# An attention and FFN kernel: the first loads in halves on two queues, and the first weight fold ahead of the transposes

## The reference

```python
x = L0_attn_X                                  # (4, 1024, 256)
xn = (x - mean) / sqrt(var + 1e-5)
s = attention(xn, Wq, Wk, Wv, Wo)              # 16 heads of 16, rope, causal softmax
x1 = fwht(xn * SU_ug) / 64                     # Walsh-Hadamard over 256
x_up = x1 @ W_up.T * (Wscale_ug[:1024] * 64)
x_gate = x1 @ W_gate.T * (Wscale_ug[1024:] * 64)
h = fwht(silu(x_gate) * x_up * SU_dp) / 64     # over 1024
g = silu(h @ W_down.T * (Wscale_dp * 64))
out = x + s * g
```

## Time and profile before

| | |
|---|---|
| median of 3 runs | 826.0 us (824.46 to 828.24) |
| the profiled execution | 825.88 us |
| its span, first to last instruction | 824.1 us |
| TensorE busy | 785.3 us, 95% |
| VectorE, ScalarE, GpSimd busy | 563.7, 497.7, 416.8 us |
| HBM read, written | 57.54, 36.95 MB |

### The profile page before, as it was taken

How to read it: one execution, slowest core, us unless ns; L and a number is a source line. 1 busy time by engine, 2 the same in 40 slices (tenths; PEclk the granted TensorE clock), 3 DMA queues, 4 the chain that set the end, 5 groups by cost and what they waited for, 6 DMA issues and landing times.

```text
span 824.1 us, 14501 instructions
## 1 busy us (share of the span) xinstructions
PE 785.3 (95%) x5212; PEld 479.7 (58%) x5212; DVE 563.7 (68%) x1019; ACT 497.7 (60%) x684; POOL 416.8 (51%) x474
## 2 busy tenths in 40 slices
PE   3999999999998999999999999999999999999987
PEld 2678888888765555554555555555555555554435
DVE  3785555445367777777777777777777777776736
ACT  2455475363543667666676765777766677666562
POOL 4569848476580553411665434166453236745233
PEclk9999999999999999999999999999999999999999
DMA  9144442463541221333334453334344333445121
GB/s 322 52 154 128 154 157 78 142 183 131 192 93 52 54 76 53 103 92 118 84 86 118 132 170 99 92 106 128 105 119 139 98 103 98 123 127 182 50 95 58
DMA packets 61055, 95.71 MB, mean 116 GB/s; under 512 B 10360, under 2 KB 27448, under 8 KB 60984
## 3 DMA queue, kind: packets, MB, share of 16 engines
q1 hardware_dynamic: 59400, 92.94, 37.2%
q10 hardware_dynamic: 1584, 1.84, 0.7%
HBM read 57.54 MB, written 36.95 MB: 115 GB/s over the span
## 4 chain that ended last, share of the span: by engine, by line
PE 62%; DVE 5%; POOL 2%; ACT 1%; DMA 1%; issue 1%; SPq 0%; DVEq 0%; ACTq 0%; POOLq 0%
PE ps L1361 15%; PE ps L327 12%; PE ps L1339 11%; PE ps L1316 10%; PE ps L337 7%; PE ps L1402 3%; DVE ps L1615 2%; PE ps L1327 2%; DVE mx L1620 2%; POOL a_sb L382 1%; DMA scr_heads<-o_raw 1%; ACT y_sb L362 1%; DVE y_sb L374 1%; DMA q_s<-shift 0%; ACT a_sb L347 0%
## 5 line engine op out<-in xcount | busy, mean ns | idle before, releaser
L1504 ACT ACTIVATE probs<-ps 128x1024 f32<-128x1024 f32 (+1 forms) x320 | 291.5, 937 | 108.2 <-PE ps L1339 106.4
L1620 DVE TENSOR_REDUCE mx<-ps 128x4 f32<-128x512 f32 (+1 forms) x192 | 215.5, 1134 | 76.9 <-PE ps L1316 48.1
L1199 POOL TENSOR_SCALAR_AFFINE_SELECT probs<-probs 128x256 f32<-128x256 f32 (+1 forms) x192 | 92.8, 486 | 262.1 <-ACT probs L1504 261.0
L1615 DVE CUSTOM_DVE_ANT_0 ps<-ps,tri 128x384 f32<-128x384 f32 (+1 forms) x256 | 154.6, 647 | 30.8 <-PE ps L1316 30.4
L1361 PE MATMUL ps<-probs,v_ones 128*32 128x512 f32 (+3 forms) x1584 | 158.1, 489 | 0.3
L1339 PE MATMUL ps<-q_s,k_s 64*128 64x512 f32 (+3 forms) x768 | 143.5, 399 | 8.1 <-DVE mx L1615 2.3
L1316 PE MATMUL ps<-k_s,q_s 48*128 48x512 f32 (+3 forms) x768 | 137.2, 382 | 3.4 <-DVE mx L1620 1.6
L1339 PEld LDWEIGHTS ps<-q_s,k_s 64*128 64x128 f32 x768 | 68.2, 185 | 104.8 <-issue 69.0
L1316 PEld LDWEIGHTS ps<-k_s,q_s 48*128 48x128 f32 x768 | 69.3, 184 | 70.9 <-ACT probs L1504 50.0
L327 PE MATMUL ps<-xh,wug_hi 128*128 128x512 f32 x256 | 105.7, 413 | 3.7 <-DVE rot L850 1.9
L382 POOL TENSOR_TENSOR a_sb<-a_sb,u_sb 128x512 f32<-128x512 f32 x64 | 83.2, 1307 | 40.3 <-ACT u_sb L355 21.5
(11 more groups left out here) (145 smaller groups left out, 1050.7 us busy)
## 6 DMA issues: line engine op xcount, KB each, us to landing
scr_qk<-kinds SPq DMA_DIRECT2D x64, 256.0 KB, 2.5
q_s<-scr_qk SPq DMA_DIRECT2D x64, 128.0 KB, 2.8
k_s<-scr_qk SPq DMA_DIRECT2D x64, 128.0 KB, 3.0
scr_heads<-o_raw SPq DMA_DIRECT2D x30, 256.0 KB, 2.1
x_sb<-in_x SPq DMA_DIRECT2D x8, 512.0 KB, 5.5
scr_v<-v_st SPq DMA_DIRECT2D x16, 256.0 KB, 2.9
q_s<-scr_qk SPq DMA_DIRECT2D x64, 64.0 KB, 3.0
k_s<-scr_qk SPq DMA_DIRECT2D x64, 64.0 KB, 3.0
```

The lines of the kernel that those rows point to most:

```text
L1199: pool.affine_select(out=part, in_=part, compare_op=ALU.is_ge, fill=0.0, base=0, pattern=pattern, channel_multiplier=-1).then_inc(cut, 1)
L1504: act.activation(probs[:, n % 2, p, :, 0:w], ps[:, bank:bank + 2, 0:w], ACT.Exp, scale=SCALE).then_inc(exp_ok, 1)
L1615: last = dve.tensor_tensor_reduce(part_of, part_of, sh.tri[:, CH - w:CH], 1.0, LOWEST, ALU.add, ALU.max, mx[:, v % 2, kind, h, i % TPC:i % ...
L1620: last = dve.tensor_reduce(out[:, :, pairs[0]:pairs[0] + n], ps[:, banks[0]:banks[0] + 2, 0:n * w].rearrange('p e (x k) -> p e x k', x=n), ...
```

## The change

Fold 0 moves ahead of the transposes of chunk 0; fold 1 stays behind them. Every load of x is issued as two halves of two token rows each, and every load of a part of `wug` as two halves, one for each block of 128 input features. For chunk 0 and part 0, SyncE issues one half and ScalarE the other, ScalarE ahead of its loads of `wqkv`; all other halves are SyncE's. The semaphores of these loads are awaited at 32 instead of 16. ScalarE normalises chunk 0 before it rounds the first `wqkv` piece, and rounds fold 0 ahead of x's high part. VectorE takes fold 0's low terms ahead of x's low part, and fold 1's ahead of the rest of `wqkv`.

```diff
--- before.py
+++ after.py
@@ -101,12 +101,12 @@
 NUG, NW = (4, 6)
 PART = 2 * INTER // NUG
 UG_PARTS = (2, 0, 3, 1)
-FOLDS = {(-1, 0): (0, 1), (0, 0): (2,), (0, 2): (3,), (1, 1): (4,), (1, 2): (5,)}
+FOLDS = {(-1, 0): (0,), (-1, 1): (1,), (0, 0): (2,), (0, 2): (3,), (1, 1): (4,), (1, 2): (5,)}
 folds_at = lambda k, place: FOLDS.get((k, place), ())
 part_done = lambda kind, ib: UG_PARTS.index((ib * P + (INTER if kind == 'gate' else 0)) // PART) + 1
 
 
-sequence = [('X', 0)] + [('W', i) for i in folds_at(-1, 0)]
+sequence = [('W', i) for i in folds_at(-1, 0)] + [('X', 0)] + [('W', i) for i in folds_at(-1, 1)]
 for k in range(NCHUNK):
     for place, turn in enumerate((('Q', k), ('K', k), ('X', k + 1), ('V', k))):
         sequence += [turn] if turn != ('X', NCHUNK) else []
@@ -453,16 +453,18 @@
         v_ok, v_taken = (sem('v_ok'), sem('v_taken'))
         block = ctx.enter_context(nc.Block())
 
+        halves = (slice(0, TPC // 2), slice(TPC // 2, TPC))
+
+        def load_x(eng, k, part):
+            eng.dma_start(x_sb[:, k % 2, part], x_d[ORDER[k]][:, part]).then_inc(x_in[k % 2], 16)
+
+        def load_ug(eng, i, d):
+            src = io['wug'].rearrange('(c p) n -> p c n', p=P)
+            part = UG_PARTS[i]
+            eng.dma_start(wug[:, i, d], src[:, d, part * PART:(part + 1) * PART]).then_inc(ug_in[i], 16)
+
         @block.sync
         def _(eng):
-
-            def load_x(k):
-                eng.dma_start(x_sb[:, k % 2], x_d[ORDER[k]]).then_inc(x_in[k % 2], 16)
-
-            def load_ug(i):
-                src = io['wug'].rearrange('(c p) n -> p c n', p=P)
-                part = UG_PARTS[i]
-                eng.dma_start(wug[:, i], src[:, :, part * PART:(part + 1) * PART]).then_inc(ug_in[i], 16)
 
             def load_table(half):
                 cols = slice(half * CH, (half + 1) * CH)
@@ -486,22 +488,27 @@
                 eng.dma_start(dst.rearrange('g p t n -> p g (t n)'),
                               v_st[:, n].rearrange('p g t n -> p g (t n)')).then_inc(sh.v_out[n], 16)
 
-            load_x(0)
+
+            load_x(eng, 0, halves[0])
             eng.dma_start(had[:, :], io['had']).then_inc(had_in, 16)
+            load_ug(eng, 0, 0)
             eng.dma_start(scales[:, :], io['scales']).then_inc(scales_in, 16)
-            load_ug(0)
-            load_ug(1)
-            load_x(1)
+            for d in range(DC):
+                load_ug(eng, 1, d)
+            for part in halves:
+                load_x(eng, 1, part)
             load_table(ORDER[0] % QC)
-            load_ug(2)
-            load_ug(3)
+            for i in (2, 3):
+                for d in range(DC):
+                    load_ug(eng, i, d)
             load_table(1 - ORDER[0] % QC)
             for k in range(NCHUNK):
                 if k:
                     store_kinds(k - 1, 1)
                 if k + 2 < NCHUNK:
                     eng.wait_ge(xt_ok, k + 1)
-                    load_x(k + 2)
+                    for part in halves:
+                        load_x(eng, k + 2, part)
                 if k == 6:
                     eng.wait_ge(ones_set, 1)
                     for which in range(2):
@@ -667,7 +674,7 @@
                 if i < NUG:
 
                     pe.wait_ge(had_ok, 1)
-                    pe.wait_ge(ug_in[i], 16)
+                    pe.wait_ge(ug_in[i], 32)
                     for o in range(DC):
                         pe.matmul(ps[:, bank + o, :], had[:, :], wug[:, i, 0, :], start=True, stop=False)
                         last = pe.matmul(ps[:, bank + o, :], (minus_had if o else had)[:, :], wug[:, i, 1, :], start=False,
@@ -683,9 +690,10 @@
                 for i in folds_at(k, place):
                     fold_weights(i)
 
+            folds(-1, 0)
             pe.wait_ge(ident_ok, 1)
             transposes(0)
-            folds(-1, 0)
+            folds(-1, 1)
             for k in range(NCHUNK):
                 pe.wait_ge(wq_ok, 1)
                 pe.wait_ge(xh_ok, k + 1)
@@ -713,7 +721,7 @@
         def _(act):
 
             def normalise(c):
-                act.wait_ge(x_in[c % 2], 16 * (c // 2 + 1))
+                act.wait_ge(x_in[c % 2], 32 * (c // 2 + 1))
                 act.wait_ge(centred, c + 1)
                 for t in range(TPC):
                     last = act.activation(x_sb[:, c % 2, t, :], x_sb[:, c % 2, t, :], ACT.Identity,
@@ -759,15 +767,19 @@
                                        su_dp_s[:, ib:ib + 1])
                 last.then_inc(w_hi, 1)
 
+            load_x(act, 0, halves[1])
+            load_ug(act, 0, 1)
             src = io['wqkv'].rearrange('(c p) n -> p c n', p=P)
             act.dma_start(wqkv[:, :, 0:2 * D], src[:, :, 0:2 * D]).then_inc(qkv_in[0], 16)
             act.dma_start(wqkv[:, :, 2 * D:], src[:, :, 2 * D:]).then_inc(qkv_in[1], 16)
             act.dma_start(wd[:, 0], io['wd'].rearrange('(c p) n -> p c n', p=P)).then_inc(d_in, 16)
+            normalise(0)
             act.wait_ge(qkv_in[0], 16)
             act.copy(wqkv_hi[:, :, 0:2 * D], wqkv[:, :, 0:2 * D]).then_inc(wq_hi, 1)
-            normalise(0)
+            for i in folds_at(-1, 0):
+                weights_high(i)
             take_xh(0)
-            for i in folds_at(-1, 0):
+            for i in folds_at(-1, 1):
                 weights_high(i)
             act.wait_ge(qkv_in[1], 16)
             act.copy(wqkv_hi[:, :, 2 * D:], wqkv[:, :, 2 * D:]).then_inc(wq_hi, 1)
@@ -816,7 +828,7 @@
         def _(dve):
 
             def variances(c):
-                dve.wait_ge(x_in[c % 2], 16 * (c // 2 + 1))
+                dve.wait_ge(x_in[c % 2], 32 * (c // 2 + 1))
                 for t in range(TPC):
                     last = dve.bn_stats(stats[:, t, :], x_sb[:, c % 2, t, :])
                 last.then_inc(stats_ok, 1)
@@ -904,11 +916,13 @@
             dve.wait_ge(scale_ok, 3)
             dve.tensor_tensor(sh.half_both[:, :], sh.half_gate[:, :], ws_ug[:, 0:IB], op=ALU.mult).then_inc(scales_ok, 1)
             weights_rest(0)
+            for i in folds_at(-1, 0):
+                weights_low(i)
             take_xl(0)
             variances(1)
+            for i in folds_at(-1, 1):
+                weights_low(i)
             weights_rest(1)
-            for i in folds_at(-1, 0):
-                weights_low(i)
             for k in range(NCHUNK):
                 if k:
                     kinds_low(k - 1, 1)
```

## The result

The changed kernel takes 821.11 us, median of 7 runs (819.32 to 823.89), against 826.46 of 7 runs (824.11 to 828.68) of the kernel before: a ratio of 0.9942, with a 95% interval of 0.9921 to 0.9964. That is 5.35 us between the medians and 4.8 by the ratio; the forecast was 4.5. A second set on another occasion (12 runs of it, 17 of the kernel before) gave 0.9955 (0.9936 to 0.9973), 4.2 us between the medians. The gain is about 0.5% of the time, small but outside both intervals. The profiled execution took 821.92 us, with a span of 820.2.

What follows compares the result with a forecast made beforehand. TensorE, busy 95% of the span, bounds the kernel, with VectorE's chain releasing the first gate: TensorE gains 5.0 us, the gate 4.5, so 825.88 - 4.5 = 821.4, with the median 0.1 above: 821.5 us, range 818.7 to 825.2.

Steps and rivals of the forecast that it cites:

- the waits at the port: VectorE waiting behind GpSimd at the shared SBUF port before the first FFN gate: about 4.1 us before, 2.8 forecast.
- x: Opening loads: x, halved over two queues, lets VectorE's statistics begin at 5.3 instead of 6.43, a gain of 1.1 us.
- Fold 0's start: TensorE's opening: fold 0 starts at 7.6 instead of transposes at 12.59, 5.0 us earlier (4.3 to 6.0).
- Length of fold 0: TensorE's opening: 6.4 slow passes and 1.6 fast ones take 6.2 us, ending at 13.8 (12.8 to 14.5).
- The clock: TensorE's whole span: granted clock reads full throughout, so only an earlier start or moved waits can matter.
- What Q needs: Chunk 0: x's low part ends at 17.9, 0.2 us ahead of TensorE; moving the low terms forward costs nothing.
- The normalisation: ScalarE, chunk 0: normalised x is there at 11.3, before fold 0 is over, so the transposes don't wait.
- The down weights: `wd` on ScalarE's queue lands at 18.0 (16.9 to 19.2); `turn(0, 1)` follows 11.1 us later, at 29.1 against 32.35.
- VectorE's chain to the gate: VectorE from `turn(0, 1)` at 29.1 to the end of `turn(1, 0)` at 44.9: 15.8 us, against 17.07 before.
- The wait at 49.48: TensorE at the first FFN gate, waiting for `turn(1, 0)`: 2.4 us instead of 1.86, gates starting at 45.0.
- Rival 3: Before the first FFN gate: port waits, or the wait there, go away; gain 5.5 to 6.9 us, 819.9 us; chance 0.20.
- Passing it on: After 49.5 us all work is released by other work, so the 4.5 us gain passes to the end whole.

Runs made afterwards that it cites:

- low terms late: Changed kernel, but VectorE takes fold 0's low terms behind the rest of `wqkv`, as the kernel before did: 826.86 us, ratio to the kernel before 1.0004.
- down weights last: Changed kernel, but the load of `wd` is issued last on SyncE's queue instead of by ScalarE: 824.25 us, ratio to the kernel before 0.9995.
- loads alone: The change's halved loads on two queues, with the kernel before's order (transposes first, then both folds): 824.62 us, ratio to the kernel before 0.9995.
- matrix behind: Changed kernel, but SyncE issues the Hadamard matrix behind its half of part 0 instead of ahead: one run, no time given, first gate at 45.38.
- rstd first: Changed kernel, but GpSimd computes rstd and shift of chunk 1 ahead of its first down fold: 822.24 us, ratio to the kernel before 0.9945.
- low terms ahead of the fold: Kernel with chunk 1's rstd ahead of GpSimd's down fold, plus VectorE taking part 3's low terms before its last down fold: one run, 823.46 us.

## Why the prediction was right

The sign and the path were right: TensorE's work moved ahead by what fold 0 moved, and the gate hung on `wd`, GpSimd and VectorE. The time (821.1 against 821.5) is nearer than the working behind it. Two terms were mis-sized, the rate of the queues and the waits at the port, and only the second reached the gate, where the gain was 5.6 us and not 4.5. In the medians it was 5.35, and the kernel before came out 0.46 us slower in these seven runs than in the three from which I started; the second set gave 4.2. That 821.1 lies within 0.4 of the forecast is in part luck.

- **x.** Statistics forecast at 5.3, seen at 4.79: both queues gave their 256 packets at the pace of bytes or better. In the eleven other profiles with this load on two queues they began at 4.45 to 5.31, and with x whole on one queue at 6.31 and 6.43. The Trainium skill's rule ("DMA: Bandwidth & Descriptors", "Issuing engines are not separate DMA queues"), taken alone, would have left x at 6.43. The trace agrees with it that the engines are shared, since 4 to 7 us moved no more in sum; what the second queue changed was what stood ahead of x.
- **Fold 0's start: mis-sized.** I had 7.6 and part 0 at 7.1. `minus_had` was there at 7.01, earlier than forecast, but part 0 landed at 8.4. The term that failed is the queues' rate: I took it from 4 to 8 us of the kernel before (0.36 MB a us), and it was 0.25. TensorE's own gain was 4.0 us instead of 5.0. At the gate this cost nothing, since the gate was released by VectorE: it only shortened TensorE's wait there.
- **Length of fold 0.** 6.2 forecast, 6.29 seen. In the eleven other profiles in which it stood first it took 5.2 to 6.5, inside the bounds of 5.2 and 6.9; that one profile agrees to 0.1 is luck. The Trainium skill, "TensorE: Matmul & The Clock Gate", Part 1, says that the number of slow matmuls at a kernel's start differs from run to run; these profiles agree.
- **The clock.** I read the row of nines as full speed throughout. It isn't: the kernel before has 7 us at the lower level near 800, and the changed kernel's first profile the stretch at 246 besides.
- **What Q needs.** x's low part ends at 18.89 and Q is listed at 19.03. Its second matmul follows fold 1's last pair by 1.09 us, as before (1.08): nothing lost, the cover of 0.2 held. What I didn't see is that the low terms' place decides the start of fold 2 too (4.0 us of wait with the low terms late): I priced their cost and not their need.
- **The normalisation.** I had x normalised at 11.3; it was at 11.7, with ScalarE's table load of 1.28 us in front, which my sum left out. With fold 0 until 14.84 it was covered.
- **The down weights.** 18.0 forecast, 18.44 seen; 11.1 us from there to `turn(0, 1)` forecast, 11.12 seen. With the down weights last the one moved and the other followed.
- **VectorE's chain to the gate: mis-sized.** I had 15.8 us with 2.8 of port waits; it took 14.3. I had named the right operations and laid them out one by one, with one price too high: rstd held VectorE for 1.0 us in my list, between the two halves of the down fold. In the trace the halves took 1.21 us each, back to back from 35.76 to 38.10. It was rstd that waited, for the first half: it took 1.93 us instead of 1.02 and ended at 37.85, while the second half ran. The other 0.5 us are lengths taken too long, 0.3 of it a port wait of `minus_mean` inside the statistics that I took from the kernel before (0.44 us instead of 0.17).
- **Why the down fold met no rotation.** GpSimd's second rotation of K ended at 35.74, and the down fold began at 35.76, free. That is no near miss. `minus_mean`, which stands two operations ahead of it, came at 34.79, while that rotation ran, and was held to its end; rstd can't start before `var_eps`, which comes behind `minus_mean`; so the down fold is the first at the port. In six more profiles `minus_mean` or `var_eps` took this wait, and the down fold took 2.35 each time. Where both small operations get through as the first rotation of K begins (before, loads alone, matrix behind), the down fold meets both rotations and takes 4.53 or 4.54. With the matrix behind, `minus_mean` came at 33.78 and the rotation at 33.91. With rstd first, `var_eps` is held by the first rotation, the down fold by the second, and it takes 3.53.
- **The wait at 49.48.** 2.4 us forecast, 0.31 seen (0.84 in the second profile). The difference is the 1.0 us by which TensorE began late and the 1.1 by which VectorE was early. Rival 3 is thereby the nearer account of the mechanism (gain 5.5 to 6.9 at the gate; it was 5.56 and 5.39), at its lower edge.
- **Passing it on.** I let the shift pass whole. It does wherever the clock reads full, up to 746 us in the second profile; each stretch of 3.4 us at the lower level takes 1.7. At full clock the time shows 4.4 us of the 5.4 to 5.6, with two runs only on the one side; where the rest goes wasn't followed up.

## What to carry to other kernels

Work that needs only weights fills the time in which activations are still being loaded and normalised. It costs a slow start nothing extra (10.6 us from TensorE's first matmul to the end of fold 1 in the first profile of either order), but it moves PSUM banks, and whoever empties them has to move too (4.0 us of wait where that was left out). A load on a second queue is worth what it overtakes: list what is pushed back, and follow that to the next wait. Where two engines meet at a shared port, lay out every operation of both lists, the small ones too, since one of 4 columns decided here who came first; or give the price as a range: starting one engine 1.4 us earlier moved the end 1.1 us later. And a wait can cost more than its length: behind waits of 3.3 and 4.0 us TensorE went on at half its clock.

## What the runs showed of the hardware

- Halved loads of `wug` started early went slowly: 227 to 298 GB/s from 4 to 7 us in both profiles of the changed kernel, with the DMA engines 82% busy or more, against 349 to 385 in the same microseconds of the kernel before, and against 346 to 387 when its own reads of `wug`, in whole parts, began at 7 us. Neither the number of queues, nor small packets, nor the first piece of `wqkv` beside it explains it.
- VectorE's large operations with both inputs in SBUF don't overlap GpSimd's large ones: `kinds_low` ended 1.07 to 1.09 us behind `queries_low` in all fourteen profiles. "SBUF — State Buffer" of the Trainium skill names the lock; that even a 4-column operation (`minus_mean`, 0.98 us instead of 0.17) waits for it wasn't in my sum.
- GpSimd's rstd, of 4 columns, is held by VectorE's down fold (1.93 us instead of 1.02) but doesn't hold it. With low terms ahead of the fold, rstd ran from 36.37 to 37.39 and the down fold's first half from 36.42 to 37.65: 1.02 and 1.23 us, against 1.02 and 1.21 without the other.
- The clock fell at places that recur, and not in every profile: near 250 us in ten of the fourteen, near 755 in seven, near 800 in ten. The stretch near 250, of 3.4 us, came after two waits of 0.95 and 0.69 us that other profiles passed at full clock. In the two kernels with an added wait of 4.0 or 3.3 us, ending at 25.07 and 31.05, it was at the lower level from 25.6 for 3.4 us and from 30.1 for 6.8.
